# Attention with heads: TensorE's first mix of each run moves between the run's two blocks of scores

## The reference

```python
q, k, v = project(layernorm(x)), project(ctx), project(ctx)   # 16 heads x 8
scores = einsum('bhqd,bhkd->bhqk', q, k) / sqrt(8)
attn = softmax(scores, axis=-1)
out = einsum('bhqk,bhkd->bhqd', attn, v)
x = x + out @ wo + bo
```

## Time and profile before

| what | value |
|---|---|
| median of 3 runs | 2349.59 us (2340.85 to 2354.88) |
| profiled execution, its own time | 2356.95 us |
| its span, first to last instruction | 2355.2 us |
| mean granted TensorE clock | 0.936 |
| busy: TensorE / ScalarE / VectorE | 2115.2 / 1449.9 / 1307.6 us |

### The profile page before, as it was taken

One profiled execution on the slowest core, in us unless ns is written; L12 is line 12 of the kernel. 1 busy time (PEld: TensorE's weight loads), 2 busy tenths in 40 slices (PEclk: granted clock), 3 DMA queues, 4 the chain that ended last, 5 costly groups with the idle time before them and its releaser, 6 DMA issues. The chain is left out here.

```text
span 2355.2 us, 42618 instructions
## 1 busy us (share of the span) xinstructions
PE 2115.2 (90%) x16862; PEld 1384.8 (59%) x16862; DVE 1307.6 (56%) x1796; ACT 1449.9 (62%) x1808; POOL 234.8 (10%) x305
## 2 busy tenths in 40 slices
PE   5877989989989689999948999997988999996999
PEld 3554755846748456666635666664655666664554
DVE  4553344343343576667558777755457766643333
ACT  2334456455464478888827888884428888884341
POOL 1006033041240310000000000001010000000000
PEclk9997998989989889999968999997989999997999
DMA  5858446355464487887318788732027778832000
GB/s 196 235 178 316 159 171 236 118 191 197 151 228 152 141 201 183 196 183 185 94 35 199 185 185 197 181 83 66 1 45 187 184 184 195 185 79 73 0 8 7
DMA packets 119756, 352.81 MB, mean 150 GB/s; under 512 B 20160, under 2 KB 54846, under 8 KB 118942
## 3 DMA queue, kind: packets, MB, share of 16 engines
q1 hardware_dynamic: 105774, 322.41, 50.3%
q0 software_dynamic: 13776, 27.54, 3.8%
HBM read 257.58 MB, written 91.23 MB: 148 GB/s over the span
## 5 line engine op out<-in xcount | busy, mean ns | idle before, releaser
L964 ACT ACTIVATE a_probs<-a_score 128x1200 f32<-128x1200 f32 x768 | 857.7, 1169 | 149.3 <-PE a_score L875 149.3
L875 PE MATMUL a_score<-a_qstack,a_kstack 128*128 128x400 f32 x2304 | 551.7, 372 | 9.8 <-DVE a_kstack L1025 7.7
L875 PEld LDWEIGHTS a_score<-a_qstack,a_kstack 128*128 128x128 f32 x2304 | 379.5, 190 | 179.8 <-issue 129.5
L837 PE MATMUL a_numer<-a_probs,a_v 128*18 128x200 f32 (+1 forms) x9216 | 471.6, 335 | 0.0
L837 PEld LDWEIGHTS a_numer<-a_probs,a_v 128*18 128x18 f32 (+1 forms) x9216 | 229.0, 97 | 184.0 <-issue 88.5
L1025 DVE TENSOR_TENSOR a_kstack<-a_kraw,a_kstack 64x2888 fp32r<-64x2888 f32 x96 | 303.8, 3164 | 5.1 <-ACT a_kstack L931 1.8
L1020 DVE CAST a_kstack<-a_kraw 128x2888 fp32r<-128x2888 f32 x90 | 149.8, 1665 | 12.8 <-DVE a_own L1081 9.0
L1033 DVE TENSOR_TENSOR a_qstack<-a_qrep,k_groupmask 128x1600 fp32r<-128x1600 f32 x48 | 87.5, 1824 | 121.7 <-PE a_score L875 121.2
L1680 PEld LDWEIGHTS f0r_ph<-f0r_xsT,f0r_w 128*128 128x128 f32 x896 | 119.4, 199 | 30.6 <-issue 12.5
L1680 PE MATMUL f0r_ph<-f0r_xsT,f0r_w 128*128 128x128 f32 x896 | 123.5, 283 | 9.2 <-DVE f0r_xsT L1868 9.2
L2080 ACT ACTIVATE f_hidden<-f_ph,f_b 128x400 f32<-128x400 f32 x128 | 75.8, 593 | 88.6 <-PE f_ph L2004 80.8
(11 more groups left out here) (358 smaller groups left out, 2725.1 us busy)
## 6 DMA issues: line engine op xcount, KB each, us to landing
a_kraw<-keys SPq DMA_DIRECT2D x384, 361.0 KB, 7.0
values<-kv_vst SPq DMA_DIRECT2D x32, 1296.0 KB, 5.2
a_v<-values SPq DMA_DIRECT2D x48, 864.0 KB, 5.8
keys<-kv_made SPq DMA_DIRECT2D x48, 722.0 KB, 5.2
l0a_ctxT<-in_ctxT SPq DMA_DIRECT2D x16, 722.0 KB, 7.8
kv_ctxT<-in_ctxT SPq DMA_DIRECT2D x16, 722.0 KB, 8.5
l0a_ctx<-in_ctx SPq DMA_DIRECT2D x16, 704.0 KB
l0a_mask<-in_mask_BxSxS_ik SPq DMA_DIRECT2D x16, 564.1 KB
```

Source lines behind the costliest of these rows:

```text
L837: last = pe.matmul(numer[32 * g:32 * g + PC, p * 2 * SQ:(p + 1) * 2 * SQ], v[0:rows(t), j, t, (2 * g + p) * PC:(2 * g + p + 1) * PC], prob ...
L875: last = pe.matmul(to, kstack[:, j, g * SK + t * 128:g * SK + (t + 1) * 128], qstack[:, j, g * GH:(g + 1) * GH, :], start=True, stop=not s ...
L964: act.activation(probs[:, n % NP, :].rearrange("p (g q) -> p g q", g=SPAN), slot_ps[:, n % 2, :, 0:GQ], ACT.Exp, scale=HSCALE).then_inc(ex ...
```

## The change

In each run the first of its mixes is issued after the first three scores, ahead of the second three; the others stay behind the second three (and behind lines 901 and 907, where a run has these). In run 0 the mixes are those of the batch before. The mixes after the last batch come in the same order as before, with no scores between. Nothing else is changed.

```diff
--- before.py
+++ after.py
@@ -891,8 +891,15 @@
                         if shifted:
                             maxima(b)
                     for i in range(SLOTS // 2):
+                        if i == 0:
+                            at, parts = b - 1, range(3 * (SLOTS // 2) - 4, PAIRS * KT) if b else ()
+                        else:
+                            at, parts = b, range(max(3 * i - 4, 0), 3 * i - 1) if b < B else ()
                         if b < B:
                             scores(b, 2 * i, shifted)
+                        for x in parts[:1]:
+                            mix(at, x // PAIRS, x % PAIRS)
+                        if b < B:
                             scores(b, 2 * i + 1, shifted)
                         if i == 1 and b:
                             pe.wait_ge(own_ready, b)
@@ -907,13 +914,8 @@
                                 last = pe.matmul(misc[0:SQ, 256:256 + D], att[:, p, :], wo2[:, p, :],
                                                  start=(p == 0), stop=(p == PAIRS - 1))
                             last.then_inc(y_full, 1)
-                        if i == 0:
-                            if b:
-                                for x in range(3 * (SLOTS // 2) - 4, PAIRS * KT):
-                                    mix(b - 1, x // PAIRS, x % PAIRS)
-                        elif b < B:
-                            for x in range(max(3 * i - 4, 0), 3 * i - 1):
-                                mix(b, x // PAIRS, x % PAIRS)
+                        for x in parts[1:]:
+                            mix(at, x // PAIRS, x % PAIRS)
 
             pe.wait_ge(cleared, 3)
             pe.wait_ge(flag_ready, 1)
```

## The result

The changed kernel takes **2469.5 us** (median of 4 runs, 2461.6 to 2473.3) against 2350.0 us before: 1.051 times as long, 95% interval 1.047 to 1.055. The forecast was 2466 us.

What follows compares the result with a forecast made beforehand. TensorE was taken to set the pace, with ScalarE waiting for it. The terms 122 - 23 + 17 gave +116 us on the 2349.59 us median, so 2466 us; own range 2444 to 2488, with 2440 to 2490 holding some 8 in 10.

Steps and rivals of the forecast that it cites:

- Block changes: TensorE's blocks: splitting scores and mixes adds a pair of blocks, 0.32 us each, 381 times: +122 us.
- Waits for the exp: Second three scores on TensorE: their waits for ScalarE's exp all go, 0.47 us a batch, 48 batches: -23 us.
- The new wait: First mix of a batch, moved earlier, waits for VectorE's numer_free: 0.39 us, 45 times: +17 us.
- terms 1 and 3: The extra pairs of blocks (+122 us in all) and the moved first mix's wait for numer_free (+17 us in all).
- Edits at nothing: Exp ring places, VectorE's time, layer 2's masked values, key and value loads, lines 901 and 907: no cost.
- ScalarE's idle time: Sign of being right: ScalarE's idle before line 964 goes up from 149 to about 265 us.
- changing blocks for nothing: Rival at the two new block boundaries: gaps overlap with other work, -6 us, 2344 us; chance 0.03.
- half the pair: Rival: a score block's first weight load is pulled ahead, a split costs 0.15 us, +51 us, 2401 us; chance 0.05.
- a flag in time: Rival at a batch's first mix: numer_free arrives in time, so no wait there, +99 us, 2449 us; chance 0.09.
- the clock: Rival: more gaps in TensorE's work bring back 1.2 GHz at times, up to 100 us more, 2566 us; chance 0.05.
- the prediction's estimate: Two drains of about 128 cycles (0.053 us) a pair: +35 us, 2385 us; set aside for the profile rows.

Runs made afterwards that it cites:

- run 4: No follow-up: one of a batch's eight runs in the kernel, each six scores and then its mixes; median 2.43 us before the change, 2.75 us after.
- two fp32 extras: Kernel before plus 384 unread fp32 matmuls of 100 columns within the second three scores: 2425.5 us with 128 weight columns, 2525.5 us with 18, against 2368.0 us.
- strip extra: Kernel before plus 384 unread fp32 matmuls of 18 weight columns, 100 columns streamed, after the first score of every second slot: 2525.5 us against 2368.0 us.

## Why the prediction was right

It was right in the sign, the size and the terms. By its own steps:

1. *Block changes, +122 us.* A run without waits is now 2.75 us, 2.77 forecast before rounding; one mix alone takes 0.46 us, 0.48 taken from the line through two and three. Run 4 hardly waits before or after, and its median over 48 batches goes from 2.43 to 2.75 us: 381 splits at 0.32 us are 122 us. That it belongs to the form of the matmul, argued from the earlier trace rows, is shown by the two fp32 extras.
2. *Waits for the exp, -23 us.* 155 such waits became 3. Before, the medians of the runs 2, 5 and 7 were 2.59 us against the 2.43 of run 4; with all three at run 4's length the batch gains 0.47 us, 23 us in all. The 15 us that the splits of runs 5 and 7 returned by themselves are two thirds of it.
3. *The new wait, +17 us.* 45 times, 0.66 - 0.27 = 0.39 us each, 17.6 us; taking it out with its split gave 35 us back against the 32 of terms 1 and 3.
4. *Edits at nothing.* VectorE's busy time is the same, its waits for key loads in the stages are 2.5 us before and after, and the only new wait of TensorE of any size is that for numer_free. The list does put 335 gaps ahead of mixes down to an exp, 91.4 us in all, but at 0.27 us each they have the length of a plain boundary.

Sum: 116 forecast, 117.6 in the stages, 119.5 in the medians. A batch was to be 23.3 us and is 23.30.

What was off: ScalarE's idle time was to rise to 265 us and rose to 224.4. The stages did grow by as much, but the exps' busy time rose by 43 us as pairs stopped overlapping; I had taken it as fixed. It costs nothing as ScalarE isn't the bound.

The rivals: changing blocks for nothing, half the pair and a flag in time are all refuted by the timeline above, and the clock stayed at 0.99. The Trainium skill (TensorEngine Tiling (Array Packing), Key Properties) names the drain between tiling modes; the trace agrees in kind. With the drain's length from TensorE: Matmul & The Clock Gate (Part 2, the drain step) of the Trainium skill, the prediction's estimate was 2385 us, 85 us under what was measured; the rows' price of 0.32 us a pair decided, and it was right to take it. What a pair pays beyond a drain was not measured.

What stays open: what the 0.32 us of a pair are made of, and why 18 columns in fp32r open no gap where 18 in fp32 do.

## What to carry to other kernels

Read what a boundary costs before putting work into a wait: two or three block lengths in the timeline of weight loads give a price per item and a price per block, and the second was here 0.32 us against a wait of 0.15 us in three runs of eight. Matmuls of the form that already stood on both sides filled such a wait at no cost here (2351.9 us against 2350.3), but gained nothing either, as the wait is set by another engine's chain from the run's start and came back in the next run. When a step moves earlier, check every semaphore it waits for against its new time: here it met numer_free, in another order the exps.

## What the runs showed of the hardware

- Going from 128 x 128 matmuls to strips of 32 columns, and back, leave TensorE's loads idle for 0.26 and 0.33 us. The gap alone is not the price: it is shorter behind matmuls of fewer columns (0.13 us ahead of the mixes behind line 907's 128 columns, in run 3 of the kernel before; 0.16 behind the strip extra's 100). What a pair costs on the path is the 0.32 us of the blocks. Going from 128 to 36 rows within strips costs 0.12 us (a block of four mixes takes 1.60 us with it and 1.48 without). A change from fp32r to fp32 of the same form costs nothing that can be seen.
- An fp32r matmul with only 18 weight columns opened no gap: it stands among full-width ones as one of them.
- The gap goes with the granted clock. At the start of the first stage of the kernel after, TensorE's loads stand idle for 2.98 us ahead of the first score and 1.11 us ahead of the seventh. From 836 to 842 us the granted clock is then 0.50 (the 1.2 GHz level), and the gaps are 0.47 and 0.65 us instead of 0.26 and 0.33:

```profile
838.00:840.00 2.00, 2.00 (x15) 0.99 (x11) 0.98 (x2) 1.07 (x2) 0.00 (x0) 0.50 1.04 220
840.00:842.00 2.00, 2.00 (x19) 0.99 (x11) 1.97 (x2) 1.07 (x2) 0.00 (x0) 0.50 1.00 205
```

```profile
839.51 0.16 PEld L837 LDWEIGHTS a_numer<-a_probs,a_v 128*18 128x18 f32 x8 [0.47 <-issue]
840.32 0.83 PEld L875 LDWEIGHTS a_score<-a_qstack,a_kstack 128*128 128x128 f32 x3 [0.65 <-issue]
```

- The same kernel before took 2350 us in three of the four comparisons here and 2368 on the chip of the fourth. Absolute times from different chips aren't to be compared.
